# A set-attention graph layer on one core: the edge search moved from ahead of the main loop into it

## What is computed

```python
h = x @ w_lin + b_lin
msg = h[edge_src]
pos = jnp.arange(e) - starts[edge_dst]
dense = jnp.zeros((n, max_deg, d), h.dtype).at[edge_dst, pos].set(msg, mode='drop')
mask = jnp.zeros((n, max_deg), bool).at[edge_dst, pos].set(True, mode='drop')
xb = _mab(dense, dense, *enc, mask)
xp = jax.nn.relu(xb @ pma_lin_w + pma_lin_b)
p = _mab(seed, xp, *pma, mask)
dd = _mab(p, p, *dec)
out = jax.nn.relu(jnp.nan_to_num(dd).reshape(n, d))
...
x = _layernorm(x + out)
```

## Time and profile before

| | us |
|---|---|
| median of 3 runs | 4284.98 (4283.5 to 4286.52) |
| the profiled execution | 4279.91 |
| its span | 4278.1 |
| busy: PE, POOL, DVE, ACT | 3488.9, 3155.2, 2677.3, 1391.3 |
| first node gather starts | 275.4 |
| last node gather ends | 4196.9 |
| DMA, mean | 62 GB/s |

### The profile page before, as it was taken

How to read it: one execution, slowest core, us unless ns; L and a number is a source line. 1 busy time by engine, 2 the same in 40 slices (tenths; PEclk the granted TensorE clock), 3 DMA queues, 4 the chain that set the end, 5 groups by cost and what they waited for, 6 DMA issues and landing times.

```text
span 4278.1 us, 111348 instructions
## 1 busy us (share of the span) xinstructions
PE 3488.9 (82%) x43804; PEld 2153.5 (50%) x43804; DVE 2677.3 (63%) x5467; ACT 1391.3 (33%) x2596; POOL 3155.2 (74%) x3353
## 2 busy tenths in 40 slices
PE   3716888888888888888888888888888888888887
PEld 1414555555555555555555555555555555555554
DVE  6744566666666666666666666666666666666665
ACT  0202333333333333333333333333333333333332
POOL 5777777777777777777777777777777777777771
PEclk9999999999999999999999999999999999999998
DMA  5633222222222222222222222222222222222230
GB/s 156 198 104 75 55 54 54 54 54 55 54 55 55 54 55 54 54 55 54 54 54 54 55 54 55 54 55 55 54 55 55 54 55 54 54 55 54 57 77 17
DMA packets 166583, 264.92 MB, mean 62 GB/s; under 512 B 95221, under 2 KB 109526, under 8 KB 166102
## 3 DMA queue, kind: packets, MB, share of 16 engines
q0 software_dynamic: 111328, 239.45, 21.0%
q1 hardware_dynamic: 54806, 18.27, 1.9%
HBM read 247.88 MB, written 11.23 MB: 61 GB/s over the span
## 4 chain that ended last, share of the span: by engine, by line
POOL 55%; issue 24%; PE 14%; DMA 5%; DVE 2%; POOLq 1%; ACT 0%; ACTq 0%; DVEq 0%
POOL gathered L578 52%; DMA gathered<-node_table,idx 3%; PE ps L688 3%; PE ps L651 3%; PE ps L669 2%; PE ps L704 2%; PE ps L723 1%; POOL xp_rows L544 1%; PE ps L753 1%; POOL gathered L544 1%; PE ps L727 1%; PE ps L763 1%; PE ps L745 1%; DVE hT L883 0%; POOLq L113 0%
## 5 line engine op out<-in xcount | busy, mean ns | idle before, releaser
L578 POOL DMA_INDIRECT gathered<-node_table,idx x3136 | 2966.1, 946 | 955.8 <-issue 939.0
L651 PE MATMUL ps<-ident,gathered 128*128 128x128 f32 x3136 | 526.1, 317 | 539.0 <-DMA gathered<-node_table,idx 538.4
L1071 DVE SCALAR_TENSOR_TENSOR xb<-ps,cols,h 128x512 f32<-128x512 f32 x392 | 294.3, 751 | 1020.4 <-PE ps L723 1020.2
L651 PEld LDWEIGHTS ps<-ident,gathered 128*128 128x128 f32 x3136 | 439.8, 211 | 633.5 <-issue 430.8
L772 ACT ACTIVATE xp_rows<-ps 128x512 f32<-128x512 f32 x392 | 234.1, 597 | 1184.2 <-PE ps L745 1184.2
L772 ACT ACTIVATE qT<-ps 128x512 f32<-128x512 f32 x392 | 234.1, 597 | 1052.3 <-PE ps L651 1052.3
L1126 DVE STREAM_TRANSPOSE probs_diag<-probs 32x512 f32<-32x512 f32 x784 | 550.9, 703 | 29.0
L669 PE MATMUL ps<-xb,pma_diag 128*128 128x512 f32 x784 | 478.6, 697 | 0.0
L688 PE MATMUL ps<-probs_diag,gathered 128*64 128x128 f32 x6272 | 454.9, 290 | 0.3 <-DVE h L993 0.3
L688 PEld LDWEIGHTS ps<-probs_diag,gathered 128*64 128x64 f32 x6272 | 359.1, 145 | 179.3 <-issue 169.5
L723 PE MATMUL ps<-h,ff_diag 128*128 128x512 f32 x784 | 440.7, 644 | 0.8 <-ACT xp L813 0.4
(11 more groups left out here) (184 smaller groups left out, 3324.2 us busy)
## 6 DMA issues: line engine op xcount, KB each, us to landing
gathered<-node_table,idx POOLq DMA_INDIRECT x3136
node_table<-hT SPq DMA_DIRECT2D x14, 448.0 KB, 4.4
qT<-in_x SPq DMA_DIRECT2D x13, 224.0 KB, 5.4
rows<-in_x SPq DMA_DIRECT2D x24, 112.0 KB
out_rows<-rows SPq DMA_DIRECT2D x20, 104.0 KB
gathered<-in_dst,win_idx POOLq DMA_INDIRECT x98, 4.2
xp_rows<-src_padded,sidx POOLq DMA_INDIRECT x98
src_padded<-in_src SPq DMA_DIRECT2D x1, 1562.5 KB, 15.9
```

What stands on the lines that cost most here:

```text
L578: pool.indirect_dma_start(out=gathered[:, s.slot(0, RING), t * ROW:(t + 1) * ROW], out_offset=None, in_=table, in_offset=bass.IndirectOffs ...
L651: mm = pe.transpose(ps[:, bank, p * P:(p + 1) * P], gathered[:, s.slot(0, RING), lo:lo + 2 * ROW - 1:2], ident[:, :])
L1071: V.scalar_tensor_tensor(xb[:, s.slot(L_FF, 2), :], ps[:, B_FF, :], c_("ff_b", P), h2[:, s.slot(L_FF, 2), :], ALU.add, ALU.max).then_inc(x ...
```

## The change

- **Search in the loop.** 1250 samples (every 320th), loaded as 125 x 10 single integers, spread to all partitions by PE (a product of ones with a diagonal). A window table in DRAM holds, per sample, 352 entries of dst and 352 of src beside each other (2816 bytes). Per iteration POOL makes one gather from it. VectorE finds the offset by two counts over 352, and moves src down by that offset with nine predicated copies, one per bit; a 32 x 32 transpose gives the indices. idx_all is gone: idx has two halves, each good for four octets.
- **First three searches** read dst and src themselves, two gathers each, since the window table is built only behind the node table. Two of them run during the table.
- **Counts** per iteration: PE folds them (two small products in the step of the scores), VectorE copies them out.
- **Table.** x is loaded once to rows, 97 nodes on a partition, so node numbers lie differently on partitions; the weights are multiplied together first, so that a turned x needs one product of 64 rows per 128 nodes; chunks of four tiles, ScalarE copies the even tiles and VectorE the odd ones; 16 staging slots in gathered. The bias of h moves into later biases, that of the query into the copy to qT.
- **Output**: one DMA per part. 391 octets, and the last has 5 tiles.

```diff
-SAMPLES = 625
-HALF = 7
-CHUNK = 7
+SAMPLES = 1250
+SAMPLE_TILES = 10
+CHUNK = 4
+STAGED = 16
+DIRECT = 3
...
+        WIN = STRIDE + DEG
...
+            for c in range(CHUNKS):
+                sp.wait_ge(tab_even, c + 1)
+                sp.wait_ge(tab_odd, c + 1)
+                if c < CHUNKS - 1:
+                    sp.dma_start(by_partition(table)[:, c * CHUNK:(c + 1) * CHUNK, :],
+                                 staged[:, c % STAGED, :].rearrange("p (m n) -> p m n", m=CHUNK)
+                                 ).then_inc(tab_out[c // 8], 16)
...
+                sp.dma_start(win_table[0:whole, c * WIN:(c + 1) * WIN],
+                             bass.AP(tensor=edges.tensor, offset=0, ap=[[STRIDE, whole], [1, WIN]])
+                             ).then_inc(table_in, 16)
...
+            for u in range(DIRECT - 1):
+                gather_direct(u)
+            for i in range(len(tab_out)):
+                stored = 2 if i == len(tab_out) - 1 else 8
+                pool.wait_ge(tab_out[i], 16 * stored)
...
+                if s.has_iteration(-6) and (s.looped or s.at >= 2):
+                    u = s.iteration(-6)
+                    wait_apart(pool, idx_ready, u - 1, pool_passed)
...
+                        gather_windows(u, s.slot(-6, RING) // OCTS_PER_IT,
+                                       lambda sem_, count_: wait_apart(pool, sem_, count_, pool_passed))
                 wait_apart(pool, av_ps, s.octet(RING - 1), pool_passed)
-                wait_apart(pool, idx_ready, s.octet(-1), pool_passed)
-                for t in range(OCT):
+                if s.has_iteration(0):
+                    wait_apart(pool, idx_ready, s.iteration(0) + 1, pool_passed)
+                for t in range(tiles_of(s.octet(0))):
...
+            def search(u, h, rounds):
+
+                direct = 2 - h if not isinstance(rounds, int) else min(rounds + 1, 2 - h)
+                dve.wait_ge(win_in[h], rounds * 16 + (16 + 16 * direct))
...
+                V.tensor_scalar(flags[1][:, :], dst_win, node, None, ALU.is_lt, ALU.add, accum_out=below[:, :]
+                                ).then_inc(found, 1)
+                V.tensor_scalar(flags[2][:, :], dst_win, node, None, ALU.is_le, ALU.add, accum_out=upto[:, :]
+                                ).then_inc(found, 1)
...
+                for b in reversed(range(BITS)):
+                    far = min((1 << b) - 1, WIN - (1 << b)) + DEG
+                    V.copy_predicated(src_win[:, 0:far], below_bits[:, b:b + 1].broadcast_to((P, far)),
+                                      src_win[:, 1 << b:(1 << b) + far]).then_inc(shifted, 1)
+                    wait_apart(dve, shifted, u * BITS + (BITS - b), dve_passed)
+                V.transpose(idx[:, h, :], src_win[:, 0:DEG]).then_inc(idx_ready, 1)
...
+            for c in range(CHUNKS):
+                table_odd(c)
+                if c == 6:
+                    search(0, 0, 0)
+                if c == 9:
+                    search(1, 1, 0)
+                if c == 12:
+                    V.memset(probs_diag[:, :, :, :], 0.0)
...
-                if s.has(0):
-
-                    if s.looped or 1 <= s.at <= OCTETS - RING:
-                        dve.wait_ge(g_in[s.slot(1, RING)], s.round(1) * (16 * OCT) + 16 * OCT)
-                        V.tensor_copy(idx[:, s.slot(1, RING), :], idx_all[:, bass.ds(s.octet(1 - RING) * OCT, OCT)]
-                                      ).then_inc(idx_ready, 1)
+                if s.has_iteration(-5) and (s.looped or s.at >= 3):
+                    for lag in (3, 2, 1, 0):
+                        dve.wait_ge(g_in[s.slot(lag, RING)], s.round(lag) * (16 * OCT) + 16 * OCT)
+                    search(s.iteration(-5), s.slot(-5, RING) // OCTS_PER_IT, s.round(-5))
+                if s.has_iteration(-11) and (s.looped or s.at >= 1):
+                    rows_of(s.iteration(-11), s.slot(-11, RING) // OCTS_PER_IT)
```

More of the change, by code:

```diff
@@ L542, in gather_windows @@
-            def gather_windows(table_ap, size, index, target, h, landed):
-                for t in range(HALF):
-                    pool.indirect_dma_start(
-                        out=target[:, h, t * size:(t + 1) * size], out_offset=None, in_=table_ap,
-                        in_offset=bass.IndirectOffsetOnAxis(ap=index[:, h, t:t + 1], axis=0),
-                    ).then_inc(landed[h], 16)
-            for h in range(2):
-                pool.wait_ge(win_idx_ready, h + 1)
-                gather_windows(dst_rows, WINDOW, win_idx, windows, h, win_in)
@@ new lines, in turn_x @@
+            def turn_x(c):
+                last = min((c + 1) * CHUNK, ITS)
+                for i in sorted({part_of(m) for m in range(c * CHUNK, last)}):
+                    pe.wait_ge(x_in[i], 16)
+                wait(pe, x_copied, c - 1)
+                for k in range((last - c * CHUNK) // 2):
+                    m = c * CHUNK + 2 * k
+                    mm = pe.transpose(ps[:, c % 2, k * P:(k + 1) * P],
+                                      rows[:, m:m + 2, :].rearrange("p m d -> p (m d)"), ident[:, :])
+                mm.then_inc(x_turned, 1)
@@ L858, in _ @@
+            V.memset(consts[:, :], 0.0)
+            V.memset(windows[:, :, 2 * WIN:2 * WIN + DEG], 0)
+            for b in range(BITS):
+                V.memset(bit_of[:, b:b + 1], 1 << b)
             V.memset(seed_u[:, :], 0.0)
-            V.memset(starts[:, ITS:ITS + 1], float(E))
             V.memset(eps[:, :], EPS)
-            V.memset(rows[:, ITS - 1, :], 0.0).then_inc(dve_zero, 1)
-            dve.wait_ge(pool_cst, 2)
+            dve.wait_ge(pool_cst, POOL_CONSTS)
             V.tensor_copy(iota_j[:, :], iota_ji[:, :])
-            link(V.tensor_copy(node_f[:, :], node_i[:, :]))
@@ L903, in _ @@
-            rows_of_group(1, 1)
+            for q in range(QUADS):
+                last = V.tensor_scalar(node_f[DEG * q:DEG * q + DEG, :], node_i[DEG * q:DEG * q + DEG, :],
+                                       float(-(QUADS * DEG - 1) * FULL * q), None, ALU.add)
+            link(last)
+            for q in range(QUADS):
+                last = V.tensor_scalar(node_f[DEG * q:DEG * q + DEG, FULL:ITS], node_i[DEG * q:DEG * q + DEG, FULL:ITS],
+                                       float(-(P - 1) * q), None, ALU.add)
@@ L1141, in y_rows @@
                 if s.at == L_Y:
-                    dve.wait_ge(rows_in, ROWS_LOADED)
+                    for i in range(len(x_in)):
+                        dve.wait_ge(x_in[i], 16)
                 m = s.iteration(L_Y)
```

641 lines of the change are left out of this document (315 added, 326 removed).

## The result

The changed kernel takes **4191.6 us** (median of 4 runs, 4188.5 to 4195.2) against 4285.2 of the kernel before (4 runs, 4283.5 to 4286.5): a ratio of **0.978, 95% interval 0.977 to 0.980**, 94 us less. The forecast was 4218, the range 4190 to 4262; the time lies 1.6 us above its low end. The profiled execution took 4192.8, 1.8 more than its span.

What follows compares the result with a forecast made beforehand. POOL's evenly paced gathers were taken as the bound: start 92 + gathers 4029.1 + hold 10 + tail 80 = 4211.1 us of span, plus 1.8 and 5.1 gives 4218. Range 4190 to 4262.

Steps and rivals of the forecast that it cites:

- The start: Time before the first node gather: 92 us instead of 275.4, bounds 67 and 105.
- Samples: Load of 1250 single integers at the start: landing between 12.5 and 24.2 us, taken as 18.
- product, passes, copy and counts: VectorE and PE steps in series behind the samples: 13.3 us together, so VectorE's share of the table begins at 31.
- The table: PE's node table chunks before the first gather: 23 chunks at 2.4 us, ten passes of 0.24 each, 55 us.
- PE's waits for the searches and the clearing: During the table, searches and clearing sit between VectorE's copies; beyond PE's slack 3 us show.
- Rival 1: Short start: PE at 0.15 a pass in the table, or samples at 12.5; start 67 to 80, time 4193 to 4206; chance 0.22.
- The gathers: POOL's loop: 3125 node plus 97 window gathers, 3222 at 1.2505 us each, 4029.1 us, 107.6 more than before.
- The hold: VectorE's copies of each search hold up POOL's gathers in the loop: 10 us in all, bounds 0 and 40.
- Rival 3: Nine copies follow so closely that a gather is held through them: 167 us more, 4375; chance 0.07.
- VectorE in the loop: A search of 5.6 us per four octets, copies about 0.25 each; PE falls 3.7 behind and recovers; no cost to POOL.
- Rival 4: VectorE becomes the bound: copies of 1.0 us put PE 9.7 behind, over the 6.2 it can regain; 4560; chance 0.04.
- The tail: From the last gather to the end: 81.2 plus 2.5 for later steps minus 3.4 for fewer stores, 80 us, plus or minus 4.

Runs made afterwards that it cites:

- Run 5: Changed kernel with VectorE waiting for the samples right after its first four clearings: samples there by 4.9 us; 6684.9 us where the kernel before took 6358.
- run 6: Changed kernel with each table chunk's products issued upper half first, then lower: eight passes unchanged at 1.23 us; 6683.5 us where the kernel before took 6358.
- run 3: Changed kernel with each window gather of the loop made twice, the second into an unread tile: 4303.3 us, ratio 1.006 to the kernel before.
- runs 1 to 3: Changed kernel without the predicated copies from the third search on, 4185.8 us; with the search moved half a step on, 4185.7; with window gathers made twice, 4303.3.
- runs 4: Changed kernel with VectorE longer ahead of h: nine copies made twice, 4608.6 us, ratio 1.077; instead three wide instructions more per search, 4313.0 us, ratio 1.008.

## Why the prediction was right, and where not

**What the right time rests on.** The sum was 26.5 us too high: 25.7 at the start and 6.4 because the median lay 1.3 below the profiled execution and not 5.1 above it, less 6.0 that the tail was too short (the gathers and their hold came out 0.4 apart). The mechanism held: POOL's gathers are the loop, and the time is their count plus a short start and a tail. But three terms were off, and with the tail as predicted the time would have been 4185.6, under the range. That it lies inside is in part luck.

**The start, 25.7 us too long.** Two terms were mis-sized. Samples: they landed by 4.9, so VectorE reached them at 9.3 only because of the weights ahead, and came to its first table copy at 22.5 instead of 31 (8.5 us; product, passes, copy and counts were 13.2 of 13.3). I had scaled the 11.73 of the earlier trace rows, a load to another place beside other loads, with the number of integers. By the rule of the Trainium skill (DMA: Bandwidth & Descriptors, "Why a DMA increments its semaphore by 16 and not by 1") my estimate of the landing would have been 24.2. Run 5 bears out neither figure. The table: 43.8 from there to the first gather against 61 (17.2 us). PE worked 34 on the chunks instead of 55, most of them at 1.77 and six at 1.0 instead of all at 2.4, because the passes of 64 rows were cheaper than those of 65 that I had priced (run 6). PE's waits for the searches and the clearing were 5.4 instead of 3, and the steps before and behind 4.4 instead of 3. Rival 1 took this side, with 0.22, and the start fell 0.7 us under its lowest figure. But its reason, a PE busier than before and so at 0.15 a pass, isn't what happened: the clock was at its lower level for most of the table (0.51 from 22 to 36 us, 0.50 from 43 to 59) and the passes were 0.15 all the same. The 1.00 of the earlier trace rows says nothing of the level there, as the pace of 0.213 shows.

**The gathers, right.** 3222 of them; run 3 gives the price of one more by itself.

**The hold, right in size by chance.** I priced 10 and the loop was 9.6 over, but runs 1 to 3 show that the copies cost 1 to 2; of the 9.6, 8 go with a gather of 947 ns instead of 944. Had the execution been one of the others, the sum would have been 8 too high here as well. Beside the copies of this profile a gather took 1.00 at 2023.35, and the next one 0.94. So the rule of the Trainium skill on the shared way into SBUF (SBUF — State Buffer, "Who interferes with whom") is seen at most at a twentieth of a microsecond, where the sum had 0.05 to 0.27 for each of ten instructions. Rival 3 did not happen. Gathers over 1.3 us came only from 3959 us on, where the rows are normalised, up to 1.82; the kernel before has them there too, up to 1.71.

**VectorE in the loop, right.** A copy took 0.242 (I had 0.25), a search 5.9 (5.6; the terms as the prediction lists them, with 0.1 behind each of nine copies, add up to 5.85), PE fell 3.8 us behind (3.7). PE still waits 1.5 us per octet over the whole run (1.3 from 1000 to 3000 us), as predicted, but not where I said: per four octets it is 3.8 for h and 1.5 to 2.2 for gathers. Rival 4's turning point was 6.2 us of lag; runs 4 put it at 5.3 to 5.9.

**The tail, 6 us too short.** SP's two stores took what I gave them: 4188.08 to the end, 2.9 us, against 6.5 from 4271.55. But PE's last turn came at 4110.00, 5.1 us after the last gather's end, where it had been 2.4:

```profile
4110.00 1.23 PE L632 MATMUL ps<-ident,gathered 128*128 128x128 f32 x8
```

So PE was later by 2.7 when the gathers ended, which the sum did not have. From that turn to the end it took 81.0 where it had been 78.8, although the stores gained 3.6; so the steps behind it cost 5.9 more, not 2.5. With the search moved PE's last turn comes 3.0 behind the last gather and the tail is 84.1: most of the lateness goes with the wait for h, the 81.0 behind it stays.

## What to carry to other kernels

Count the engine that issues one thing after another at a fixed pace, and divide; a chain of waits that wanders between two nearly full engines does not name the bound. Put a late addition where its engine waits anyway, even if the time does not change: moving the search took PE's wait for h from 3.8 to 0.3 us per four octets and left that much slack. Whether the next saving needed it was not run: with one window gather for two nodes the gathers of four octets take 40.6 us, and 3.8 of wait plus 35.4 to 36.0 of work would still fit. A price per pass is read from passes with the same number of rows and at the same clock level; here 64 rows and 65 differ by a third.

## What the runs showed that I had not expected

- A wait of PE costs more than itself. After 4.2 us without work the 16 products of attention took 1.97 us and the two ff passes 2.07, against 1.10 and 1.13 later: the lower of the two clock levels. Mean clock of the changed kernel and its variants against PE's wait for h per four octets: 0.935 at 0.3, 0.916 at 3.8, 0.897 at 7.1, 0.864 at 9.8.
- Nine more copies and waits in VectorE's loop body brought a stall of 2.8 us in every pass of eight octets, with loads of instructions (1.93 MB) that the other kernels do not have.
- 1250 single integers from DRAM were there at most 4.15 us after their load was issued (4.89 less 0.74).
- Passes of 64 rows started two at a time, 0.145 us each in a group of eight, where passes of 65 and 128 rows started 0.213 apart, all at the pace of the lower clock level.
- The median gather is 944 or 947 ns, fixed within an execution and not by the kernel's text.
- On a chip where PE stalled in its small score products (1549 us against under 44), one change went from 2.2% faster to 4.6% slower.
